# Handing five of 25 products of each tile to an accumulating DMA, in a convolution kernel with a mixture of experts behind it

## The reference

```python
h    = einsum('bchw,oc->bohw', ln_c(x), reduce_w) + reduce_b
kern = einsum('bchw,oc->bohw', h, span_w) + span_b        # 49 weights per group and point
conv = (kern.reshape(b, G, 1, 49, H, W) * patches(ln_c(x), 7, 7)).sum(axis=3)
x    = x + conv
t    = tokens(x)                                          # 12544 tokens of 128 channels
t    = t + moe(ln_t(t))                                   # 8 experts, top 2, hidden 341
```

## Time and profile before

| | before |
|---|---|
| median of 3 runs | 1503.39 us (1500.45 to 1503.68) |
| the profiled execution | 1498.94 us, span 1497.1 us |
| PE, DVE, POOL, ACT busy | 83%, 75%, 74%, 39% of the span |
| granted TensorE clock, mean | 0.95 |
| last product of tile 7, last product of tile 27 | 309.8 us, 1204.3 us |

### The profile page before, as it was taken

The page is one execution under the profiler, slowest core; times in us unless marked ns, Lnnn a source line. Parts: engine busy times, 40 slices in busy tenths (PEclk is TensorE's granted clock), DMA queues, the critical chain, the costliest instruction groups (busy, mean ns, idle before and its releaser), DMA issues. The chain is left out here.

```text
span 1497.1 us, 23125 instructions
## 1 busy us (share of the span) xinstructions
PE 1243.9 (83%) x7667; PEld 1015.6 (68%) x7667; DVE 1122.8 (75%) x1663; ACT 579.5 (39%) x1960; POOL 1112.2 (74%) x788
## 2 busy tenths in 40 slices
PE   4898878788988989899899898899989887587771
PEld 2676767676766777677787777777778676465661
DVE  5998888988898998888889898888889943222220
ACT  4333333334443444444345343454434244133230
POOL 4787979784686887678788687877778875665665
PEclk9999898998999999999999999999999999899996
DMA  4111111112232242332324232243322445666652
GB/s 124 41 60 48 59 49 59 49 31 88 53 79 60 69 97 63 88 78 60 85 59 103 62 86 62 60 100 83 71 58 48 105 119 129 174 137 134 145 117 25
DMA packets 93346, 120.40 MB, mean 80 GB/s; under 512 B 11531, under 2 KB 72428, under 8 KB 93082
## 3 DMA queue, kind: packets, MB, share of 16 engines
q1 hardware_dynamic: 53802, 90.97, 20.0%
q0 software_dynamic: 39424, 27.96, 13.3%
HBM read 78.92 MB, written 42.65 MB: 81 GB/s over the span
## 5 line engine op out<-in xcount | busy, mean ns | idle before, releaser
L851 DVE TENSOR_TENSOR prod<-kern_ps,xn 128x896 f32<-128x896 f32 x592 | 627.9, 1082 | 65.7 <-PE kern_ps L586 63.2
L586 PE MATMUL kern_ps<-h_stack,span 98*128 98x448 f32 x1372 | 466.3, 426 | 112.7 <-DVE prod L851 72.1
L1088 POOL TENSOR_TENSOR acc_p<-acc_p,prod 128x896 f32<-128x896 f32 x192 | 435.9, 2270 | 74.1 <-DVE prod L851 69.4
L1109 POOL DMA_INDIRECT out<-y_tok,idx x224 | 351.6, 1570 | 137.4 <-issue 66.2
L601 PE MATMUL acc_ps<-ident_sb,prod 128*112 128x128 f32 x2864 | 388.4, 280 | 0.0
L601 PEld LDWEIGHTS acc_ps<-ident_sb,prod 128*112 128x112 f32 x2864 | 341.3, 137 | 37.9 <-DVE x L1053 7.8
L586 PEld LDWEIGHTS kern_ps<-h_stack,span 98*128 98x128 f32 x1372 | 227.1, 200 | 205.5 <-DVE prod L851 121.5
L1097 POOL DMA_INDIRECT xs<-rows_x,slots x224 | 219.0, 978 | 61.0 <-issue 41.3
L536 PEld LDWEIGHTS bank<-w2b,hid 114*128 114x128 f32 x1344 | 181.7, 202 | 50.7 <-DVE xf_lo L1046 26.0
L536 PE MATMUL bank<-w2b,hid 114*128 114x128 f32 x1344 | 190.1, 288 | 26.2 <-DVE xf_lo L1046 15.9
L780 ACT ACTIVATE silu<-h_ps 114x512 f32<-114x512 f32 x132 | 79.0, 598 | 235.0 <-PE h_ps L627 235.0
(11 more groups left out here) (154 smaller groups left out, 1349.9 us busy)
## 6 DMA issues: line engine op xcount, KB each, us to landing
wb<-wexp SPq DMA_DIRECT2D x56, 684.0 KB, 5.4
xb<-xs SPq DMA_DIRECT2D x56, 264.0 KB, 3.0
w2b<-in_w SPq DMA_DIRECT2D x56, 171.0 KB
xt<-in_x SPq DMA_DIRECT2D x28, 224.0 KB, 3.4
out<-x SPq DMA_DIRECT2D x28, 224.0 KB, 2.6
wexp<-wb SPq DMA_DIRECT2D x8, 684.0 KB, 3.2
xs<-rows_x,slots POOLq DMA_INDIRECT x224, 2.3
out<-y_tok,idx POOLq DMA_INDIRECT x224
```

Source lines behind the costliest of these rows:

```text
L586: last = mm(kern_ps[:, g % 2, i, 0:N], span[:, k * C:(k + 1) * C], h_stack[:, t % 2, :], start=True, stop=True)
L851: v.tensor_tensor(pair_rows(dst), kern.rearrange("p i (r w) -> p i r w", w=W), taps, ALU.mult).then_inc(s_prod, 1)
L1088: g_.tensor_tensor(acc_p[:], acc_p[:], prod[:, (t * TAPS + u) % PRING, :], ALU.add).then_inc(s_padd, 1)
L1109: g_.indirect_dma_start(out=out, out_offset=bass.IndirectOffsetOnAxis(ap=idx[:, b % XBRING, q:q + 1], axis=0), in_=y_tok[:, b % 2, q * C:( ...
```

## The change

From tile 8 on, five products a tile (units 1, 5, 11, 17, 20) are added to the product after them (2, 6, 12, 18, 21) by a DMA from SBUF to SBUF that accumulates, issued by POOL (`merge`). PE then sums the second of each pair only, at the earliest seven steps after its product. POOL keeps five units (0, 4, 8, 15, 22), so four adds instead of seven. DVE keeps its four. PE is left with 2, 3, 6, 7, 9, 12, 14, 18, 21, 23 and 24: eleven instead of 13. The ring gets ten slots. To make room in SBUF, two outputs that nobody reads become bf16. Tiles 0 to 7 keep their split and their places.

```diff
-BY_POOL = [tuple(range(0, 21, 2)) if t < LATE else tuple(range(0, 22, 3)) for t in range(TILES)]
+BY_POOL = [tuple(range(0, 21, 2)) if t < LATE else (0, 4, 8, 15, 22) for t in range(TILES)]
 BY_DVE = [() if t < LATE else (10, 13, 16, 19) for t in range(TILES)]
-BY_PE = [tuple(u for u in range(TAPS) if u not in BY_POOL[t] + BY_DVE[t]) for t in range(TILES)]
+BY_DMA = [() if t < LATE else (1, 5, 11, 17, 20) for t in range(TILES)]
+MERGE_NO = {(t, u): n for n, (t, u) in enumerate((t, u) for t in range(TILES) for u in BY_DMA[t])}
+MRING = 4
+def soonest(t, u):
+    return 7 if u - 1 in BY_DMA[t] else 2
+BY_PE = [tuple(sorted((u for u in range(TAPS) if u not in BY_POOL[t] + BY_DVE[t] + BY_DMA[t]),
+                      key=lambda u: u + soonest(t, u))) for t in range(TILES)]
-PRING = 8
+PRING = 10
...
-        while _left and at(_t, _left[0]) + 2 <= _S and (...):
+        while _left and at(_t, _left[0]) + soonest(_t, _left[0]) <= _S and (...):
...
-        unused = {k: sb(f"unused_{k}", [SUB, 2, SUBS, C]) for k in ("ln1", "ln2")}
+        unused = {k: sb(f"unused_{k}", [SUB, 2, SUBS, C], BF16) for k in ("ln1", "ln2")}
...
+        def merged(eng, t, u):
+            n = MERGE_NO[(t, u)]
+            eng.wait_ge(s_merge[n % MRING], 16 * (n // MRING + 1))
         def consumer(eng, t, u):
...
+            elif u in BY_DMA[t]:
+                merged(eng, t, u)
...
                     pe.wait_ge(s_prod, t * TAPS + u + 1)
+                    if u - 1 in BY_DMA[t]:
+                        merged(pe, t, u - 1)
...
+            def merge(t, u):
+                n = MERGE_NO[(t, u)]
+                g = t * TAPS + u
+                pool.wait_ge(s_prod, g + 2)
+                if n >= MRING:
+                    pool.wait_ge(s_merge[n % MRING], 16 * (n // MRING))
+                g_.dma_start(prod[:, (g + 1) % PRING, :], prod[:, g % PRING, :], accum_op=ALU.add).then_inc(s_merge[n % MRING], 16)
...
                 if 0 <= p < TILES and j in BY_POOL[p][1:]:
                     add(p, BY_POOL[p].index(j))
+                if 0 <= p < TILES and j - 1 in BY_DMA[p]:
+                    merge(p, j - 1)
```

More of the change, by code:

```diff
@@ L218 @@
     while _left:
-        while _left and at(_t, _left[0]) + 2 <= _S and (LOAD.get(_S, 0) < 1.3 or min(at(_t, _left[0]) + 5, at(_t + 1, 2)) <= _S):
+        while _left and at(_t, _left[0]) + soonest(_t, _left[0]) <= _S and (LOAD.get(_S, 0) < 1.3 or min(at(_t, _left[0]) + 5, at(_t + 1, 2)) <= _S):
             SUM_AT.setdefault(_S, []).append((_t, _left.pop(0)))
@@ L349, in build @@
         s_inner = sem("s_inner")
+        s_merge = [sem(f"s_merge{i}") for i in range(MRING)]
         s_sum = sem("s_sum")
```

## The result

The changed kernel takes 1542.71 us, median of four runs (1541.02 to 1545.3), against 1503.54 of the kernel before on the same chip: a ratio of 1.0264, 95% interval 1.0239 to 1.0289, 39 us slower. The forecast was 1488. The profiled execution took 1544.33 us, its span 1542.5, 45.4 over the span before.

What follows compares the result with a forecast made beforehand. PE and DVE were taken to hand the lead to each other in tiles 8 to 27. Terms -1.25 + 0.1 + 0.4 = -0.75 us a tile, -15 us over 20 tiles, took 1503.4 to 1488 us; range 1466 to 1532.

Steps and rivals of the forecast that it cites:

- What bounds the kernel: Tiles 8 to 27: PE bounds products 0 to 4, PE mostly 5 to 12, DVE mostly 13 to 24.
- The tail moves as a block, tiles 0 to 7 stay: After tile 27: the change leaves the tail alone, so gains or losses of tiles 8 to 27 reach the end one to one.
- Products 5 to 12: Steps 29 to 36: sums fall from 5.3 to 4.6, PE 0.7 us lighter, most of it counting; -0.6 us a tile.
- Products 0 to 4: Steps 24 to 28: sums fall from 4.15 to 4.0, all on the path; -0.15 us a tile.
- a small term: PE's clock: longer waits at steps 20 to 24, without sums, may lower it; left in the range, no size given.
- Products 13 to 24: Steps 12 to 23: sums fall from 4.55 to 3.4, a bit under half counting as DVE is nearer; -0.5 us a tile.
- x1: DVE's x1 before product 30 may wait as the sum of `acc_p` moves to step 29; +0.1 us a tile, 0 to 0.4.
- The merges: POOL's accumulating DMAs: 1.3 us issue, 5.6 us landing, DMA share about 0.70, PE's wait +0.4 us a tile.
- The budget: Time from a product to PE's merged sum: 9.5 to 9.9 us available against 8.1 needed, so 1.4 to 1.8 early.
- the first rival: Merges land late and PE stands at them: 10.3 us passes the budget, +1.45 us a tile, 1532 us; chance 0.28.
- The second (DVE the real bound): PE's freed time becomes longer waits for DVE: -3 to +3 us, 1503 us; chance 0.15.
- The third: POOL becomes the bound if a direct DMA exceeds 2.4 us; at 3 us, +58 us, 1561 us; chance 0.05.

Runs made afterwards that it cites:

- the run with the filler: Changed kernel with PE's span units of steps 14, 15, 17, 18 and 20 to 24 done twice in tiles 8 to 27; 1539.92 us, ratio 1.0270.
- The run without the late sums: Changed kernel with PE's two merged sums of products 18 and 21 left out from tile 8 on, merges still running; 1531.99 us, ratio 1.0210.
- both mended: Changed kernel with POOL adding product 9 in place of 8 and merged sums allowed seven to nine steps behind; 1513.88 us, ratio 1.0101.
- the run with the gap alone: Kernel before with its 14 sums, none on steps 20 to 24 from tile 8, ten ring slots and bf16 outputs; 1546.42 us, ratio 1.0307.

## Why the prediction was wrong

- *What bounds the kernel* held, more strictly than the forecast used it: PE in products 0 to 4, and DVE in 13 to 24, where taking sums away gave nothing (22.24 us without those of steps 20 to 24, against 22.21).
- *The tail moves as a block, tiles 0 to 7 stay*: held, 44.2 of 45.4 us lie in tiles 8 to 27.
- *Products 5 to 12*, -0.6 us: -0.61. The number fits better than its working: PE's busy time there fell by 1.38 us a tile, not by 0.7, and less than half of it counted, not most.
- *Products 0 to 4*, -0.15 us: +0.99. This is the first step that failed. I counted sums by stretch and priced each at 1.0 us. But the planner can no longer spread them (seven steps behind the product in any case, so none at 20 to 24 and five at 25 to 29), and at half clock one costs 1.91 us. I had the clock in the text, from a single wait, and left it as "a small term": it was 81 us more of half clock, at which PE does half, so some 41 us of PE work against 40 us saved. Read off the first stretch with its mean clock (0.91, before 0.99), some 15 of its 20 us more would be the clock's, an estimate; the run with the filler gave 11 of them back. The run without the late sums shows what a sum costs there: 1.28 us less at full clock for two sums. The exact division stays open: fewer sums also lower the clock.
- *Products 13 to 24*, -0.5 us: +1.82. The second step that failed is the sentence on POOL's queue, that a merge's waits "hold up only the scatter and add_rows behind it, which nobody waited for". The `rsqrt` pair of step 9 stands behind the merge of step 6 and, since 8 replaced 9, behind an add. Of the two it is the add that cost measurably: without the merges the stretch was as long (23.97 us). ACT already waited 27.6 us for that pair, in a view that I had read for DVE, PE and POOL, and not for ACT. I called POOL's load hidden because POOL had 5.3 us a tile to spare, and it still has: it waits 130 us at the merges. But almost none of that lies where the pair could use it: 2.8 us of the 130 are spent at the merge of step 6, the others at steps 2, 12, 18 and 21. By the run with one add moved in the kernel before, the order costs 16 us by itself. The forced sum on step 19 is the other part, some 10 us of this stretch. With both mended 0.57 us a tile remain (one profiled execution), not explained; the clock is a candidate, but at nearly the same clock (0.92 against 0.91) the run with the gap alone lost nothing in this stretch. By that run the -0.5 itself was not to be had either: DVE bounds this stretch, and PE's lighter load gave nothing.
- *x1*, +0.1 us: 0, no idle of DVE stands before it.
- *The merges*: issue 0.97 us median for 1.3; landing 4.9 for 5.6; DMA share 0.56 for 0.70; PE's wait 0.14 us a tile for 0.4. The budget had also counted the issue twice, since the landings of the earlier trace rows are taken from the start of the issuing instruction: 1.2 + 4.9 = 6.1 us where I had 8.1, and the first rival's 10.3 is 1.3 too high for the same reason. Over tiles 8 to 27 queue q0 took 39.4% of the 16 engines for 13.5% before, which is 2.5 us of all 16 a merge where I had taken 3.5. Other DMAs landed later beside them (the expert rows `xb` 4.5 us after their issue for 3.1, medians), and by the run without merges that cost nothing. The landing less the 2.1 us around it leaves 2.8 us for 459 KB, near the 3.0 of two operands at the plain rate, far from the 4.7 of the short pieces. The 3.1 us that I estimated from the formula of the Trainium skill (DMA: Bandwidth & Descriptors, Anatomy of one DMA) lie under the least landing, 4.2: the measurement decides.
- *The rivals*: the first (late merges, 1532) has the sign and nearly the size, and fell all the same: it decides from a landing of 7.8 us, and without merges the loss was the same. The second (DVE the real bound) asked for 2 us a tile more of PE's waits for DVE and for the same idle time of DVE; the waits rose by 1.0 us, and DVE's idle time from 108.9 to 155.8 us. The third asked for POOL without waits, and POOL waited more than before. The time was 1542.7, 11 us above the range. The rivals were all about resources; none was about the order of work and its spread, of which the change moved most.

## What to carry to other kernels

Where engines run a written-out program in lockstep, work is worth what it costs on its own step: taking it from steps with slack gave nothing here, and a constraint that makes a planner put it on given steps can cost more than the work saved. When an instruction moves in an in-order queue, list everything that now stands behind it and read who waits for those, even if the engine has idle time to spare. And a merge of sums by DMA was cheap here (one microsecond of issue, five of landing); what cost was that its late result decided where the rest had to go.

## What the runs showed of the hardware

- A DMA from SBUF to SBUF that adds 459 KB, in rows of 3584 bytes, cost GpSimd 0.97 us (median) and landed 4.9 us after the start of its issue, with the DMA engines 56% busy; it took 2.5 us of all 16 engines. The add_rows issue, an indirect DMA of 128 rows of 512 bytes, cost 1.56 us.
- Fewer matmuls did not make TensorE less busy: 799 us with 12 sums a tile and 798 with 14, since the granted clock of the stretch went from 0.96 to 0.92. A sum took 1.91 us at the lower level and 1.04 at the upper.
- Doing 180 span units twice (160 pairs of matmuls and 20 single ones more) cut half-clock time from 146 to 79 us.
